# Edge scalars in two exact float32r parts, one float32r matmul per tile and per supertile, in a two-layer graph network

## The reference, cut to what matters

```
scale    = sigmoid(edge_scalars @ W_rad.T + b_rad)       # 16 scalars an edge -> 160 factors
messages = products of x[src], the edge's four harmonics and W_ss, W_sv, W_vs, W_vv
agg      = segment_sum(messages * scale, dst)
out      = linear map of (x + agg), by L_s and L_v; residual and layer norm follow
```

```
h = silu(edge_scalars @ (Wfc1 / 4))                      # 16 -> 64
w = h @ (Wfc2 / 8)                                       # 64 -> 192
mid0..mid3 = products of w, the features f[src] and the harmonics
out = linear maps of the means of mid0..mid3 over dst, gated and added to the node's own part; layer norm
```

## Time and profile before

| | us |
|---|---|
| median of three runs | 4607.15 |
| span of the profiled execution | 5144.5 |
| its table stage, up to the first gather | 68 |
| its layer 0 from the second round on | 113 to 2440 |
| its node stage between the layers | 2440 to 2600 |
| its layer 1 | 2600 to 5050 |
| its last stage | 5050 to 5144 |

### The profile page before, as it was taken

How to read it: one execution, slowest core, us unless ns; L and a number is a source line. 1 busy time by engine, 2 the same in 40 slices (tenths; PEclk the granted TensorE clock), 3 DMA queues, 4 the chain that set the end, 5 groups by cost and what they waited for, 6 DMA issues and landing times.

```text
span 5144.5 us, 61111 instructions
## 1 busy us (share of the span) xinstructions
PE 4277.3 (83%) x12412; PEld 2600.5 (51%) x12413; DVE 3878.0 (75%) x8785; ACT 2612.5 (51%) x8195; POOL 3471.2 (67%) x3267
## 2 busy tenths in 40 slices
PE   6877877877877887887878888988988898888897
PEld 4555555555555555555644444444444444444445
DVE  5878877877878887887667777777777776777777
ACT  3545555545555555554544445545454454555554
POOL 4777777777777777777266666666666666666661
PEclk7555555555555555555889999999998899999999
DMA  7655565665565665656233333333333333333331
GB/s 250 167 166 160 166 171 159 166 169 160 167 168 161 168 167 164 168 162 166 85 85 88 84 86 84 87 82 86 87 86 82 84 84 83 87 86 85 85 86 52
DMA packets 245761, 640.14 MB, mean 124 GB/s; under 512 B 57085, under 2 KB 95407, under 8 KB 245627
## 3 DMA queue, kind: packets, MB, share of 16 engines
q0 software_dynamic: 181152, 556.66, 39.8%
q1 hardware_dynamic: 64576, 83.11, 5.3%
HBM read 618.66 MB, written 20.88 MB: 124 GB/s over the span
## 4 chain that ended last, share of the span: by engine, by line
DVE 34%; PE 27%; issue 16%; another core or an unknown queue 9%; ACT 6%; DVEq 4%; DMA 2%; POOL 2%; ACTq 0%; POOLq 0%; SPq 0%
PE ps L967 15%; DVE work L679 10%; PE ps L960 6%; DVE work L660 6%; DVE onehot L712 5%; ACT work L470 5%; PE ps L954 3%; DVE work L653 2%; DVE acc L719 2%; POOL arena L373 2%; DVE arena L719 1%; PE ps L947 1%; DVE work L699 1%; DVEq L776 1%
## 5 line engine op out<-in xcount | busy, mean ns | idle before, releaser
L373 POOL DMA_INDIRECT work<-table,srcs x1596 | 1639.5, 1027 | 796.7 <-issue 633.8
L373 POOL DMA_INDIRECT arena<-table,srcs x1596 | 1755.0, 1100 | 611.4 <-issue 516.3
L967 PE MATMUL ps<-arena,onehot 128*128 128x161 f32 x3608 | 1034.6, 464 | 507.4 <-DVE arena L685 264.4
L967 PE MATMUL ps<-work,onehot 128*128 128x384 f32 x3608 | 1345.2, 521 | 79.3 <-DVE work L706 59.1
L967 PEld LDWEIGHTS ps<-arena,onehot 128*128 128x128 f32 x3608 | 884.8, 308 | 830.3 <-issue 769.8
L470 ACT ACTIVATE work<-arena,harm 128x160 f32<-128x160 f32 (+1 forms) x3224 | 984.7, 389 | 301.0 <-DMA arena<-table,srcs 266.3
L470 ACT ACTIVATE work<-work,harm 128x96 f32<-128x96 f32 (+1 forms) x3224 | 1070.3, 415 | 22.2 <-DMA work<-table,lists 11.6
L967 PEld LDWEIGHTS ps<-work,onehot 128*128 128x128 f32 x3608 | 684.8, 199 | 631.8 <-issue 270.6
L947 PE MATMUL ps<-wrad,escal 49*128 49x320 f32 x1612 | 905.2, 707 | 0.0
L960 PE MATMUL ps<-fc,hid 128*128 128x384 f32 x1612 | 639.1, 522 | 219.2 <-ACT hid L560 124.5
L679 DVE TENSOR_REDUCE work<-work 128x256 f32<-128x768 f32 (+1 forms) x806 | 656.7, 853 | 149.6 <-ACT ps L498 85.4
(11 more groups left out here) (127 smaller groups left out, 2503.9 us busy)
## 6 DMA issues: line engine op xcount, KB each, us to landing
escal<-in_escal SPq DMA_DIRECT2D x404, 98.0 KB
arena<-table,srcs POOLq DMA_INDIRECT x1596
work<-table,srcs POOLq DMA_INDIRECT x1596
table<-work SPq DMA_DIRECT2D x49, 224.0 KB, 4.6
dst_sh<-in_dst_sh SPq DMA_DIRECT2D x52, 160.0 KB
table<-work SPq DMA_DIRECT2D x7, 784.0 KB, 4.0
acc<-in_xd SPq DMA_DIRECT2D x1, 3920.0 KB
arena<-in_xd SPq DMA_DIRECT2D x7, 560.0 KB, 4.6
```

Of the source, the lines that this page charges most:

```text
L373: pool.indirect_dma_start(out=rows[:, j, t, :], out_offset=None, in_=table, in_offset=bass.IndirectOffsetOnAxis(ap=of[:, j, t:t + 1], axis ...
L967: last = mm(bank(to)[:, 0:(MSG0, MSG1)[l]], onehot[:, b, t, :], m[:, j % 2, t, :], start=t == 0, stop=t == TPS - 1)
```

## The change

The host no longer prepares the scalars' layout beyond padding: it hands over `scalars`, where a round's 16 by 2048 values lie on 128 partitions with 256 values each. In layer 0 the chip splits each value into two parts, both of which float32r holds exactly, and keeps them in HBM (`parts_d`) for layer 1 as well:

- SP loads the raw values of a round (`load_raw`); ACT copies them to float32r, the high part (`high_part`, a copy of 128x256); DVE subtracts, the low part (`low_part`, a `tensor_tensor` of 128x256 with both inputs in SBUF); SP stores both (`store_parts`, two DMAs).
- SP's `load_escal` fetches the parts of two supertiles twice, to partitions 0 to 31 and 32 to 63, so that 97 partitions take part: high, low, high, low, and rows of ones for the bias.
- The weights are split the same way once, in the table stage, by two copies and four subtractions on DVE. POOL fills the rows of ones and zeros by three memsets.
- `radial0` becomes four float32r matmuls of 160 columns, `hidden1` one of 512 columns whose stationary side holds the hidden weights twice. `silu` becomes two ACTIVATEs of 64 partitions each.
- In the table stage SP now waits, ahead of storing tile 21, for round 0's low part, and ahead of storing tile 25 for round 1's, for round 0's stores and for round 2's raw values.

The diff, cut to its core:

```
+            def load_raw(r, b):
+                sp.dma_start(raw[:, b, :], a["scalars"][:, bass.ds(r, 1), :].rearrange("p o e -> p (o e)")).then_inc(s_raw, 16)
+
+            def store_parts(r, b):
+                for k in range(2):
+                    of_part = parts_d[bass.ds(r, 1), k * FIN:(k + 1) * FIN, :].rearrange("o f (g e) -> (o f g) e", e=SEG)
+                    sp.dma_start(of_part, parts[:, b, k, :].bitcast(f32)).then_inc(s_parts, 16)
+
+            def load_escal(l, r, c):
+                of_pair = parts_d[bass.ds(r, 1), :, c * PAIR * SUP_EDGES:(c + 1) * PAIR * SUP_EDGES].rearrange("o f (j e) -> (o f) j e", j=PAIR)
+                for copy in range(2):
+                    sp.dma_start(escal[copy * PART:(copy + 1) * PART, c * PAIR:(c + 1) * PAIR, :].bitcast(f32),
+                                 of_pair).then_inc(s_esc[l][c], 16)
...
                 if n == PARTS[4]:
+                    sp.wait_ge(s_lo, 1)
+                    store_parts(0, 0)
+                    sp.wait_ge(s_raw, 32)
+                    load_raw(2, 0)
+                if n == PARTS[4] + 4:
+                    sp.wait_ge(s_lo, 2)
+                    sp.wait_ge(s_parts, 32)
+                    store_parts(1, 1)
+                    sp.wait_ge(s_raw, 48)
+                    load_raw(3, 1)
+                if n == PARTS[5]:
                     first_loads(0)
...
+                        if l == 0 and c == 0:
+                            sp.wait_ge(s_parts, 32 * (r + 2))
+                            sp.sem_inc(s_sp, 1)
+                        sp.wait_ge(s_lin[l], r * SLOTS + (c + 1) * PAIR)
+                        load_escal(l, r + 1, c)
+                        if l == 0 and c == 0:
+                            sp.wait_ge(s_lo, r + 3)
+                            sp.sem_inc(s_sp, 1)
+                            store_parts(r + 2, k % 2)
...
+            def high_part(r, more=True):
...
+                nc.scalar.activation(parts[:, b, 0, :].rearrange("p o e -> p (o e)"),
+                                     raw[:, b, :].rearrange("p o e -> p (o e)"), ACT.Copy).then_inc(s_hi, 1)
...
+                for h in range(2):
+                    of_h = slice(h * HID, (h + 1) * HID)
+                    last = nc.scalar.activation(hid[of_h, j % 2, :].rearrange("p (k n) -> p k n", k=2),
+                                                hps[of_h, :].rearrange("p (k h n) -> p h k n", k=2, h=2)[:, h], ACT.Silu)
...
+            def low_part(r):
...
+                nc.vector.tensor_tensor(of[1], raw[:, b, :].rearrange("p o e -> p (o e)"), of[0], ALU.subtract).then_inc(s_lo, 1)
...
+                        if l == 0 and j == 1:
+                            low_part(i + 2)
...
-                pe.wait_ge(s_esc[0][j // PAIR], (i + 1) * 16)
-                for k in range(2):
-                    last = mm(rad[j % 2][:, 2 * k:2 * k + 2, :], escal[:, j, k * P:(k + 1) * P], wrad[:], start=True, stop=True)
+                pe.wait_ge(s_esc[0][j // PAIR], (i + 1) * 32)
+                for t in range(TPS):
+                    last = mm(rad[j % 2][:, t, :], escal[:, j, t * P:(t + 1) * P], wrad_r[:], start=True, stop=True)
                 last.then_inc(s_lin[0], 1)
...
-                mm(hps[:, 0:2 * P], wfc1[:], escal[:, j, :], start=True, stop=True).then_inc(s_lin[1], 1)
+                mm(hps, wfc1_r[:], escal[:, j, :], start=True, stop=True).then_inc(s_lin[1], 1)
```

More of the change, by code:

```diff
@@ L37 @@
 FIN = 16
-HALF = 32
-ERO = HALF + FIN + 1
+PART = 2 * FIN
+ONE_HI, ONE_LO = 2 * PART, 3 * PART
+ERO = ONE_LO + 1
+SEGS = P // FIN
+SEG = SLOTS * SUP_EDGES // SEGS
 HID = 64
@@ L55, in mk_gnn_resnorm_d2_gnn_r8_694f30_kernel @@
 def mk_gnn_resnorm_d2_gnn_r8_694f30_kernel(nc, a):
-    f32, bf16, i32, i16 = mybir.dt.float32, mybir.dt.bfloat16, mybir.dt.int32, mybir.dt.int16
+    f32, f32r, i32, i16 = mybir.dt.float32, mybir.dt.float32r, mybir.dt.int32, mybir.dt.int16
     ALU = mybir.AluOpType
@@ L272, in _ @@
                 load_x(k)
-            def of_pair(name, s):
-                return a[name][:, bass.ds(s, PAIR), :]
             def load_dst_sh(l, q, half):
@@ L351, in _ @@
             for t, name in WEIGHTS:
-                pool.dma_start(t[:], a[name]).then_inc(s_weights, 16)
+                pool.dma_start(t if t is wrad or t is wfc1 else t[:], a[name]).then_inc(s_weights, 16)
             nc.gpsimd.memset(zeros[:], 0.0).then_inc(s_const, 1)
@@ L620, in scale_weights @@
                     nc.vector.tensor_scalar(w, w, c, None, ALU.mult).then_inc(s_wscaled, 1)
+                dve.wait_ge(s_wscaled, len(SCALED))
+                for w, r in ((wrad, wrad_r), (wfc1, wfc1_r)):
+                    nc.vector.tensor_copy(r[:], w).then_inc(s_wsplit, 1)
+                dve.wait_ge(s_wsplit, 2)
+                for w, r in ((wrad, wrad_r), (wfc1, wfc1_r)):
+                    for rows in (slice(PART, 2 * PART), slice(ONE_LO, ERO)):
+                        nc.vector.tensor_tensor(r[rows, :], w[rows, :], r[rows, :], ALU.subtract).then_inc(s_wsplit, 1)
             def make_window_table():
@@ L634, in make_window_table @@
                 nc.vector.tensor_copy(wtab[:, :, 1, :], wtabf[:, 1, :].rearrange("p (i j) -> p i j", j=SLOTS)).then_inc(s_wtab, 1)
+            def low_part(r):
+                b = bass.ds(r & 1, 1)
+                dve.wait_ge(s_hi, r + 1)
+                of = [parts[:, b, k, :].rearrange("p o e -> p (o e)") for k in range(2)]
+                nc.vector.tensor_tensor(of[1], raw[:, b, :].rearrange("p o e -> p (o e)"), of[0], ALU.subtract).then_inc(s_lo, 1)
             table_rows(1, 13)
@@ L1184, with in_four @@
                   *((192 + 64 * d, V[d] + 1, l2v[:MS]) for d in range(3)))
-    scalars = np.concatenate([placed(FIN, EDGES_PAD, (0, 0, ea.T)), np.ones((1, EDGES_PAD), ea.dtype)])
-    def of_half(h):
-        return scalars.reshape(FIN + 1, SUPS, 2, 2, P)[:, :, :, h].reshape(FIN + 1, SUPS, 2 * P)
+    scalars = placed(FIN, EDGES_PAD + SLOTS * SUP_EDGES, (0, 0, ea.T)).reshape(FIN, ROUNDS + 1, SEGS, SEG)
+    def in_four(w, bias=None):
+        blocks = [(k * FIN, 0, w) for k in range(4)]
+        if bias is not None:
+            blocks += [(ONE_HI, 0, bias[None]), (ONE_LO, 0, bias[None])]
+        return placed(ERO, w.shape[1], *blocks)
     ins = {
```

70 lines of the change are left out of this document (53 added, 17 removed).

## The result

The changed kernel takes 4659.78 us (median of 4 runs, 4650.56 to 4665.17), the kernel before 4607.96 us beside it: a ratio of 1.0111, 95% interval 1.0096 to 1.0127. It is slower by 52 us, where 22 us were forecast. A second set of runs of the same kernel (`after_again`) gave 1.0108 (1.0093 to 1.0124).

A forecast was written before the change was run, and what follows sets the result against it. The prediction took POOL's gathers as the bound, in layer 0 wholly and layer 1 mostly, with PE second. Terms 12 + 20 + 0 + 0 + 0 - 10 = +22 us gave 4630 us; own range 4617 to 4660, range of all 4500 to 4690.

The forecast's parts named there:

- POOL is the bound: Both layers: POOL's gathers set the pace, wholly in layer 0 and mostly in layer 1, 5.62 and 5.33 us a supertile.
- 124 and 310 us of waits: Layers 0 and 1: POOL's idle time beyond the gaps of 0.305 us behind gathers, expected to be smaller after.
- the late pick-up of the earlier trace: Further visits: a PE product done at 865.9 us, taken up by ACT only at 877.81 us; cited for the PE rival, 0.34.
- means no lower than 1.10 and 1.03 us: Sign for the profile after: mean gather durations of layers 0 and 1 would not fall below these.
- Table stage, +12 us, bounds 0 to 20: Before the first gather: stores on SP's queue wait for low parts, two delays of 5 to 7 us.
- Low part, +20 us, bounds 0 to 41: Layer 0: 101 DVE subtractions of 0.34 to 0.41 us stretch gathers beside them, up to 0.25 us a round.
- DMA, 0 us, bounds 0 to 60: Both layers: added transfers find room, shares rising to 0.70 and 0.36; up to 60 us if rows arrive late.
- PE, -10 us: Layer 1: `hidden1` 0.31 us shorter at a quarter of the price per column, counting only where PE is slower than POOL.
- The eighth of layer 1 at the lower clock: Layer 1: about an eighth of the time PE ran at 1.2 GHz, slower than POOL; 31 supertiles by 0.62 us.
- The granted clock did not fall: Layer 1: a granted clock below 0.94, once PE has less to do, would show the prediction wrong.
- ACT's two additions, 0 us: High part in layer 0 and second silu in layer 1, 381 ns each, hidden; otherwise 39 and up to 133 us.

The follow-up runs named there:

- stand-in: Profile of the kernel before with its silu as two ACTIVATEs of 64 partitions, same values, used as the measure of before; ratio 0.9995, 4604.9 us.
- late_parts: The changed kernel with the stores of round 0's and 1's parts behind those of tiles 31 and 37, first fetches behind tile 41; 4645.7 us, ratio 1.0080.
- one_copy: The changed kernel with the parts fetched once instead of twice from round 1 on; 4624.6 us, ratio 1.0037.
- before_fetch: The kernel before with one more load of 160 KB, which nobody reads, for each pair of supertiles in layer 1; 4618.6 us, ratio 1.0007.
- before_both: The kernel before with the unread 160 KB load for each pair in layer 1 and silu as two ACTIVATEs; 4599.5 us, ratio 1.0000.
- pe_double: The changed kernel with every radial0 and every hidden1 matmul done twice; 4683.7 us, ratio 1.0150.

## Why the prediction was right in direction and too small

*POOL is the bound.* Held, and more strictly than I put it: in both layers, before (by the stand-in) and after, its idle time is the gap behind each gather. What the profile of before showed beyond this (124 and 310 us of waits, the late pick-up of the earlier trace rows, 12% over the runs) was that one execution. For the same reason the sign "means no lower than 1.10 and 1.03 us" failed, at 1.070 and 1.020 us, without PE having a part in it: against the stand-in's 1.063 and 0.999 us the means rose. The stages of the prediction's sum add up to 4735 us, not to some 4700; its conclusion is the same.

*Table stage, +12 us, bounds 0 to 20.* Right in mechanism and nearly in size: 14 to 16 us between the profiles, of which late_parts takes 10 us away. I had not counted the wait ahead of the second raw load (SP at 38.45, issued at 43.28 us).

*Low part, +20 us, bounds 0 to 41.* Its own price came out as forecast: the operation has 0.42 us (I had 0.34 to 0.41), each of 100 low parts met a gather, and they add 21.9 us. But the meetings of the select fell by 32 us against the stand-in, and those of the weightings rose by 17 us, so that layer 0 as a whole became 9.5 us longer (5.4 us in the profile of after_again). Leaving the low part out made layer 0 19.5 us longer (2219.5 against 2200.0 us), and leaving out the whole split changed nothing. The step that failed is to price an added operation while the others stay where they are: they move.

*DMA, 0 us, bounds 0 to 60.* This is the step that failed most. I put the added loads at nothing because the DMA engines have room, and if they cost anything, in layer 0, where the share is high. Layer 1 became 33 us longer, where the share went from 0.37 to 0.42 only, and one load less of each pair takes all of it away again (one_copy, 35 us). A load's cost didn't go by its share of the DMA engines: with the second load in the changed kernel the excess of the gathers in layer 1 is 104 us, without it 69 us. These 33 us are what the forecast of +22 us lacked; they aren't the load's alone, as before_fetch and before_both show.

*PE, -10 us.* Nothing, though PE gained more than I forecast: 0.6 us a supertile in layer 1 where PE doesn't wait, not 0.31. POOL hid all of it. The eighth of layer 1 at the lower clock, out of which I had made the term, isn't there in the stand-in, whose granted clock in layer 1 is 0.99. The Trainium skill ("FP8 and Floating Point Precision", section "TensorE Precision Notes") gave an estimate of 0.21 us for the 512 columns, and the repetition in pe_double shows 0.24 us. The granted clock did not fall, 0.98 in layer 1.

*ACT's two additions, 0 us.* Held for the high part in so far as ACT never makes POOL wait; no run leaves it out alone. The second silu is free in before and worth 17 us in the change, and these are among the microseconds that one copy less saves too. The bound for it was 400 x 0.38 = 152 us by the row that it names, not 133.

With the three rows of the table for the terms: 14 + 10 + 33 us, where I had 12 + 20 - 10. That the sign was right is partly luck: the largest part was not in the sum at all.

What is shown: the time is made by POOL's gathers, the excess is in gathers that begin beside two-input operations of DVE, and one fetched copy less removes layer 1's part. What stays open is why the second copy, or a load of its size, shifts DVE against the gathers in the changed kernel by more than in the kernel before. Neither the bytes, nor the packets, nor ACT's second instruction explains it alone, and the float32r product was not tested alone. Rows that land later are an obvious path: from the end of a supertile's last gather to ACT's first weighting it is 2.18 us on average in the change and 1.95 us in one_copy. But the stand-in, whose gathers are short, has 2.26 us. That path is thus argued against by its own number, and not settled.

## What to carry to other kernels

First find the engine whose gaps are only its own issue, and add that gap to its busy time: here the engine with 73% was the bound, and the one with 90% was not. Where the bound is lengthened by meetings with another engine, an edit elsewhere acts by moving those meetings, to either side; the operation's own meetings can be forecast (21.9 us here, where 20 were), but the answer of the others has no sign that can be had from a sum of durations, and the range of the term should be as wide as the excess that the bound now carries (70 to 100 us in layer 1 here, near 180 in layer 0). A profile that lies 12% over its runs is to be checked against a second one, of the same kernel or of a harmless variant.

## What the runs showed of the hardware that was not expected

- A gather begun during a DVE operation with two SBUF inputs was longer by what was left of that operation less 0.12 us (453 gathers of the changed kernel begun during a select, to within 0.02 us), and by nothing beside an operation with an input in PSUM (0.96 us beside L792). The select didn't become longer by the gather (0.68 to 0.69 us).
- Leaving out 0.42 us of DVE work a round made the kernel 0.35% slower.
- A float32r matmul of 512 columns, done a second time, added 0.24 us to PE's gapless period; float32r in place of float32, at twice the columns, took 0.6 us from it.
- 160 KB more for each pair in layer 1 of the kernel before cost 0.07% (within error); 124 KB in the changed kernel with one copy cost 0.42%.
